# Depthwise convolution in 16x4 cells, a LayerNorm centred in PSUM, and the mixer weights loaded from GpSimd's queue

## The reference

```
x  [8, 96, 64, 64] float32
h  = batch_norm1(x)                                   # per channel scale and shift
h  = depthwise conv 17x17, padding 8, 96 groups
h  = 1x1 conv (96 x 96), batch_norm2, exact gelu
h  = h * squeeze_excite(mean of h over the image)
x1 = x + gamma * h
xn = layer_norm over the 96 channels of x1, with gain and offset
out = mamba(xn) + flip(mamba(flip(xn)))               # 192 inner channels, 16 states, 4096 steps
```

## Time and profile before

| | |
|---|---|
| median of 3 runs | 5830.08 us (5827.94 to 5831.29) |
| the profiled execution | 5833.66 us, span 5831.9 us |
| mean granted TensorE clock | 0.761 of full |
| convolution ends (last copy into hs) | 513.4 us |
| pointwise: SP's first DMA | 513.67 us |
| normalise: SP's first DMA | 639.20 us |
| scan: SP's first DMA | 825.68 us |

### The profile page before, as it was taken

One profiled execution on the slowest core, in us unless ns is written; L12 is line 12 of the kernel. 1 busy time (PEld: TensorE's weight loads), 2 busy tenths in 40 slices (PEclk: granted clock), 3 DMA queues, 4 the chain that ended last, 5 costly groups with the idle time before them and its releaser, 6 DMA issues. The chain is left out here.

```text
span 5831.9 us, 75897 instructions
## 1 busy us (share of the span) xinstructions
PE 4650.0 (80%) x18020; PEld 1375.0 (24%) x18020; DVE 5255.8 (90%) x3583; ACT 3228.0 (55%) x5273; POOL 4947.2 (85%) x2349
## 2 busy tenths in 40 slices
PE   7998766777877888788788778787887878888877
PEld 5775311111111111111111111111111111111111
DVE  3322658999999999999999999999999999999998
ACT  1123755555565656655555655656556555556564
POOL 0000248999999999999999999999999999999998
PEclk9998886666677777777777777777777777777777
DMA  1011655555656666666666566665566666566666
GB/s 36 25 29 48 194 157 188 188 184 192 200 193 202 204 191 200 197 199 194 203 201 207 191 199 206 192 199 195 196 201 197 200 207 197 196 202 202 192 198 203
DMA packets 363220, 1050.78 MB, mean 180 GB/s; under 512 B 70868, under 2 KB 120294, under 8 KB 312604
## 3 DMA queue, kind: packets, MB, share of 16 engines
q1 hardware_dynamic: 354972, 1034.97, 55.5%
q10 hardware_dynamic: 8064, 14.16, 0.7%
HBM read 837.23 MB, written 211.63 MB: 180 GB/s over the span
## 5 line engine op out<-in xcount | busy, mean ns | idle before, releaser
L1405 POOL TENSOR_TENSOR hc<-hring,c_rep 128x1024 f32<-128x1024 f32 x1541 | 3599.7, 2360 | 74.7 <-DVE hring L1360 71.0
L1360 DVE TENSOR_TENSOR_SCAN hring<-decay,carry,u_ps 128x1024 f32<-128x1024 f32 x1221 | 2823.6, 2335 | 0.0
L1111 PE MATMUL u_ps<-stack_b,w_spread 48*128 48x512 bf16 x2442 | 995.4, 496 | 1005.3 <-DVE hring L1360 1001.4
L1342 DVE TENSOR_TENSOR u_ps<-u_ps,u_rep 128x1024 f32<-128x1024 f32 x1221 | 1478.0, 1211 | 72.6 <-DMA u_rep<-u_scr 55.6
L1236 ACT ACTIVATE decay<-dt_rep,w_a 128x1024 f32<-128x1024 f32 x1222 | 1396.4, 1145 | 224.4 <-DVE hring L1360 211.8
L1129 PE MATMUL y_ps<-hc,w_gather 128*32 128x512 f32 x6144 | 1131.9, 819 | 0.0
L1236 ACT ACTIVATE u_ps<-dt_rep,w_a 128x1024 f32<-128x1024 f32 x322 | 359.3, 1116 | 1102.6 <-DVE hring L1360 1102.2
L1392 POOL TENSOR_TENSOR drive_p<-u_rep,b_rep 128x1024 f32<-128x1024 f32 x322 | 760.4, 2362 | 10.1 <-DMA u_rep<-u_scr 10.1
L1360 DVE TENSOR_TENSOR_SCAN hring<-u_ps,carry,drive_p 128x1024 f32<-128x1024 f32 x321 | 752.0, 2343 | 0.0
L1111 PEld LDWEIGHTS u_ps<-stack_b,w_spread 48*128 48x128 bf16 x2442 | 144.9, 100 | 2369.6 <-DVE hring L1360 2168.7
L684 POOL TENSOR_TENSOR xs<-xc_ln,rs 96x512 f32<-96x512 f32 x64 | 89.9, 1405 | 707.1 <-ACT rs L668 693.4
(11 more groups left out here) (128 smaller groups left out, 4326.0 us busy)
## 6 DMA issues: line engine op xcount, KB each, us to landing
dt_rep<-dt_scr SPq DMA_DIRECT2D x194, 1024.0 KB, 5.8
u_rep<-u_scr SPq DMA_DIRECT2D x194, 1024.0 KB, 7.9
c_rep<-bc_scr SPq DMA_DIRECT2D x260, 512.0 KB, 4.9
b_rep<-bc_scr SPq DMA_DIRECT2D x130, 512.0 KB, 4.3
xn<-xn_scr SPq DMA_DIRECT2D x132, 384.0 KB, 5.2
y_scr<-y_sb SPq DMA_DIRECT2D x768, 64.0 KB, 2.0
xn<-xn_scr SPq DMA_DIRECT2D x132, 256.0 KB, 4.7
dt_scr<-dt_sb SPq DMA_DIRECT2D x260, 128.0 KB, 2.2
```

The lines of the kernel that those rows point to most:

```text
L1111: mm = nc.tensor.matmul(u_ps[nv % NSLOT][:, sl], w["spread"][:, q, :], upper(stack_b[drv][:, sl]), start=True, stop=True)
L1342: nc.vector.tensor_tensor(slot[:, :], slot[:, :], u_rep[r][:, b, :], ALU.mult).then_inc(drive_ready, 1)
L1360: nc.vector.tensor_tensor_scan(hring[nv % NHR][:, ::step], factor[:, ::step], term[:, ::step], carry[:, drv, nv:nv + 1], ALU.mult, ALU.add ...
L1405: nc.gpsimd.tensor_tensor(hc[nv % NHC][:, :], hring[nv % NHR][:, :], c_rep[q][:, :], ALU.mult).then_inc(c_applied, 1)
```

## The change

Three parts.

**Convolution by cells.** The output is made in cells of 16 rows by 4 columns. A stationary matrix then has 64 columns (16 rows x 4 columns of output) instead of 128, and 5 of them (`CELLS`) serve a channel in place of 9. The partitions of the input now stand for (column mod 4, 32 rows: 16 and a halo of 8 on both sides), and the four row blocks (`NCY`) lie on the free axis. Each of the 5 steps does two matmuls, for even and odd row blocks, into partitions 0 to 63 and 64 to 127 of PSUM. The band matrices need only 16 rows x 2 halves = 32 small matmuls for a batch. For this layout `x_cols` is not changed. Instead SP issues 12 DMAs for a batch: for each of the two inner row blocks two DMAs of 64 partitions, whose source is `[2 parities, 32 rows, 1024]`, and for each of the two edge blocks four DMAs of 24 partitions. Every row is 4 KB as before. The batch norm becomes 24 instructions on 64 partitions for a batch (L316), since rows outside the image need scale and shift of zero. ScalarE alone copies out of PSUM. GpSimd copies the bf16 halves of the taps (`part`), and GpSimd zeroes parts of `xraw` before the first load.

**Mixer loads.** The 62 loads go from SP's queue to GpSimd's.

**Normalise.** TensorE multiplies by `centrer` = identity - averager, so that the centred value arises in PSUM (`px`). ScalarE squares from there, and VectorE does `px * gain * rs` in one instruction and adds the offset in another. GpSimd has no work left in this block. The leads are other ones.

```diff
+CY, CX = 16, 4
+ROWS = CY + 2 * PAD
+CELLS = 2 * PAD // CX + 1
+CELL = CELLS * CX
+NCY = H // CY
+NEAR = CELLS // 2
+XC = W // CX
+XP = XC + 2 * NEAR
 YG = 4
-NYG = H // YG
+NYG = CY // YG
...
+                rows = d["x_cols"].rearrange("(a y) c b x -> a y (c b x)", a=2)
+                def load(buf, at):
+                    for q in range(NCY):
+                        first = q * CY - PAD
+                        lo, hi = max(0, first), min(H, first + ROWS)
+                        if hi - lo == ROWS:
+                            for k in range(2):
+                                sp.dma_start(xraw[buf][2 * ROWS * k:2 * ROWS * (k + 1), q, :], rows[:, lo:hi, bass.ds(at, CB * B * XH)]).then_inc(x_in[buf], 16)
+                        else:
+                            for k in range(4):
+                                to = ROWS * k + lo - first
+                                sp.dma_start(xraw[buf][to:to + hi - lo, q, :], rows[k % 2, lo:hi, bass.ds(at, CB * B * XH)]).then_inc(x_in[buf], 16)
+                sp.wait_ge(raw_zero, 1)
                 for i in range(2):
-                    sp.dma_start(xraw[i][:, :, :, :], xk[:, i * CB:(i + 1) * CB, :, :]).then_inc(x_in[i], 16)
+                    load(i, i * CB * B * XH)
...
+                pool.wait_ge(wide_ready, 5)
+                def take(s, buf):
+                    nc.gpsimd.tensor_copy(part[buf][:, :, :], upper3(wide[:, :, bass.ds(s * (CB * CELL), CB * CELL)])).then_inc(part_ready, 1)
+                take(0, 0)
+                take(1, 1)
+                with pool.Fori(0, BATCHES // 2) as i:
                     for par in range(2):
+                        pool.wait_ge(w_ready, NYG * (2 * i + par + 1))
+                        take(2 * i + par + 2, par)
...
+                def evacuate_weights(s, buf, yg, batches_before):
+                    bank = yg % 2
+                    if batches_before is not None:
+                        act.wait_ge(conv_done[buf], CB * batches_before)
+                    act.wait_ge(w_ready, NYG * s + yg + 1)
+                    src = pw[bank][:, 0:YG * CB * CELL].rearrange("p (y n o) -> p y n o", y=YG, o=CX)
+                    to = toep[buf][:, :, yg * YG * CX:(yg + 1) * YG * CX].rearrange("p n (y o) -> p y n o", o=CX)
+                    nc.scalar.copy(to, src).then_inc(w_evac[bank], 1)
...
+                        for c in range(CB):
+                            evacuate_weights(s + 1, 1 - par, c, i + par)
+                            act.wait_ge(conv_done[par], CB * i + c + 1)
+                            nc.scalar.copy(hs[:, bass.ds((CB * s + c) * B * XH, B * XH)], pc[c][:, 0:B * XH]).then_inc(h_evac[c], 1)
...
                 def batch_norm(s, buf, loads):
-                    dve.wait_ge(x_in[buf], 16 * loads)
+                    dve.wait_ge(x_in[buf], 16 * X_DMAS * loads)
                     for c in range(CB):
                         at = s * CB + c
-                        last = nc.vector.tensor_scalar(xpad[buf][:, c, :, NEAR:NEAR + XH], xraw[buf][:, c, :, :],
-                                                       scale[:, bass.ds(at, 1)], shift[:, bass.ds(at, 1)], ALU.mult, ALU.add)
+                        for h in range(2):
+                            rows = slice(64 * h, 64 * h + 64)
+                            src = xraw[buf][rows, :, :].rearrange("p q (c b x) -> p q c b x", c=CB, b=B)
+                            for k, cells in enumerate((slice(0, 1), slice(1, NCY - 1), slice(NCY - 1, NCY))):
+                                last = nc.vector.tensor_scalar(xpad[buf][rows, c, cells, :, NEAR:NEAR + XC], src[:, cells, c, :, h::2],
+                                                               scale[rows, k, bass.ds(at, 1)], shift[rows, k, bass.ds(at, 1)], ALU.mult, ALU.add)
                     last.then_inc(x_ready, 1)
...
+                        for h in range(2):
+                            last = nc.tensor.matmul(pw[bank][64 * h:64 * h + 64, r * CB * CELL:(r + 1) * CB * CELL],
+                                                    bands[:, yg * YG + r, :, :].rearrange("p a y -> p (a y)"),
+                                                    part[buf][:, h, :],
+                                                    start=True, stop=True, skip_group_check=True)
                     last.then_inc(w_ready, 1)
...
-                            for k in range(SHIFTS):
-                                n0 = (c * SHIFTS + k) * 2
-                                last = nc.tensor.matmul(pc[c][:, 0:B * XH].rearrange("p (b x) -> p b x", b=B),
-                                                        toep[par][:, n0:n0 + 2, :].rearrange("p a y -> p (a y)"),
-                                                        xpad[par][:, c, :, k:k + XH],
-                                                        start=(k == 0), stop=(k == SHIFTS - 1))
-                                if k % 2 == 1:
-                                    weights(s + 1, after[c][k // 2])
+                            for k in range(CELLS):
+                                for q in range(2):
+                                    last = nc.tensor.matmul(pc[c][64 * q:64 * q + 64, 0:B * XH].rearrange("p (f b x) -> p f b x", f=2, b=B),
+                                                            toep[par][:, c * CELLS + k, :],
+                                                            xpad[par][:, c, q::2, :, k:k + XC],
+                                                            start=(k == 0), stop=(k == CELLS - 1))
+                                if k == 2:
+                                    weights(s + 1, 1 - par, c)
                             last.then_inc(conv_done[par], 1)
...
-                for dst, src in mixer.loads:
-                    sp.dma_start(dst, src).then_inc(w_loaded, 16)
...
+            @block.gpsimd
+            def _(pool):
+                for dst, src in mixer.loads:
+                    pool.dma_start(dst, src).then_inc(w_loaded, 16)
...
+                        b, f, x = g // GPB, g % GPB // 4, g % 4
                         last = nc.tensor.transpose(pt[g % 2][0:C, r * P:(r + 1) * P],
-                                                   hs[:, :].rearrange("p (c n) -> p c n", c=C)[:, :, 4 * g + r], ident[:, :])
+                                                   hs[:, :].rearrange("p (c n) -> p c n", c=C)[:, :, (f * B + b) * XC + 4 * x + r], ident[:, :])
...
-                    nc.scalar.activation(act_out[b % 2][:, :, 8 * col:8 * col + 8].rearrange("c y x -> c x y"),
-                                         pp[g % 2][0:C, :].rearrange("c (x y) -> c x y", y=H), ACT.Gelu,
+                    f, x = col // 4, col % 4
+                    nc.scalar.activation(act_out[b % 2][:, 32 * f:32 * f + 32, 16 * x:16 * x + 16].rearrange("c y (r o) -> c r y o", o=CX),
+                                         pp[g % 2][0:C, :].rearrange("c (r y o) -> c r y o", r=4, o=CX), ACT.Gelu,
                                          bias=bt[:, 3:4], scale=bt[:, 2:3], accum_out=sums[:, g:g + 1]).then_inc(gelu_done, 1)
...
+                dve.wait_ge(ln_const, 64)
+                nc.vector.tensor_tensor(centrer[:, :], one[:, :], averager[:, :], ALU.subtract).then_inc(centrer_made, 1)
...
-                def centre(b, s):
+                def scale(b, s):
                     r = s % RING
-                    dve.wait_ge(mean_ready, NS * b + s + 1)
-                    dve.wait_ge(added, NS * b + s + 1)
-                    after(dve, scaled, NS * b + s - RING + 1)
-                    nc.vector.tensor_tensor(xc[:, r, :], x1[:, r, :], pm[s % NM][0:C, :], ALU.subtract).then_inc(centred, 1)
-                def gain(b, s):
+                    dve.wait_ge(rs_ready, NS * b + s + 1)
+                    after(dve, affine, NS * b + s - RING + 1)
+                    nc.vector.scalar_tensor_tensor(xs[:, r, :], px[s % NX][0:C, :], lng[:, 0:1], rs[:, r, :],
+                                                   ALU.mult, ALU.mult).then_inc(scaled, 1)
+                def shift(b, s):
                     r = s % RING
                     dve.wait_ge(scaled, NS * b + s + 1)
                     after(dve, stored[r], 16 * (NS // RING * b + s // RING))
-                    nc.vector.tensor_scalar(xo[:, r, :], xs[:, r, :], lng[:, 0:1], lng[:, 1:2], ALU.mult, ALU.add).then_inc(affine, 1)
-                over_slices(dve, (4, add), (3, centre), (0, gain))
+                    nc.vector.tensor_scalar(xo[:, r, :], xs[:, r, :], lng[:, 1:2], None, ALU.add).then_inc(affine, 1)
+                over_slices(dve, (5, add), (1, scale), (0, shift))
...
+                def centre(b, s):
                     pe.wait_ge(added, NS * b + s + 1)
-                    after(pe, centred, NS * b + s - NM + 1)
-                    nc.tensor.matmul(pm[s % NM][0:C, :], averager[:, :], x1[:, s % RING, :], start=True, stop=True).then_inc(mean_ready, 1)
+                    after(pe, scaled, NS * b + s - NX + 1)
```

(19 more changed lines are left out.)

169 lines of the change are left out of this document (86 added, 83 removed).

## The result

The changed kernel takes 5912.7 us (median of 4 runs, 5912.16 to 5913.1), the kernel before 5830.68 us in the same session: a ratio of 1.014, 95% interval 1.0127 to 1.0153. It is slower by 82 us. The forecast was 5896 us.

What follows compares the result with a forecast made beforehand. Before, TensorE bounds the convolution; after, two DMA engines carrying the inner loads were to. 5833.7 + 104 (convolution) - 21 (pointwise) - 17 (normalise) = 5899.7, less 3.6 for the median: 5896 us; 5875 to 5955 holds eight in ten.

Steps and rivals of the forecast that it cites:

- Two DMA engines for the inner loads: Convolution loads: the source's outer dimension of 2 leaves each inner load two DMA engines, at 26 GB/s each.
- The convolution's term, +104: Convolution: 26 batches at 23.0 us, set by the loads, start the next stage at 617.8 instead of 513.67 us.
- For a batch each of them moves 4 x 32 + 8 x 2 = 144 packets: Convolution loads: each of the two DMA engines moves 0.59 MB, 22.7 us at 26 GB/s, taken as 23.0.
- rival (2): Convolution loads: slower packets, 19.3 GB/s as with all 16 engines, 205 us more, 6101 us; chance 5%.
- TensorE's batch, 10.5 us: Convolution: TensorE needs about 10.5 us for a batch, the matmuls for the two PSUM halves overlapping.
- rival (4): Convolution: TensorE at 1.2 GHz while waiting for loads; 21 us still hides behind 23, changing nothing; chance 2%.
- VectorE's batch, 6 us: Convolution: VectorE's 24 instructions for a batch take 6 us beside TensorE, 10 us at most.
- rival (1): Convolution: inner loads get many DMA engines, TensorE sets 10.5 us for a batch, 5576 us in all; chance 10%.
- every engine idle for two periods: Sign at the convolution's end: SP waits for x_in with every engine idle for two periods (23 us each).
- Pointwise, -21: Pointwise: ScalarE's stall of 18.42 us and slow groups behind it go, -21 us; GpSimd's queue costs 0 to +31.
- Normalise, -17: Normalise: 64 slices each 0.27 us shorter, -17 us, between -25 and +5.
- I take 2.27: Normalise: 2.27 us for a slice against 2.54 before, chosen since DMA then runs at 260 GB/s.

Runs made afterwards that it cites:

- experiment 1: Changed kernel with each inner load of 64 rows (source 2 x 32) issued as two loads of 32 rows, one parity each: 5536.96 us, ratio 0.949.
- experiment 3: Changed kernel with the first edge block's four loads of 24 rows each cut into 23 rows and 1: 6267.46 us (one run).
- experiment 8: Changed kernel without the edge blocks' loads in the loop, made for the first two batches only: 5822.49 us, ratio 0.9984 to the kernel before.
- experiment 5: Kernel before with only the 62 mixer loads moved from SP's queue to GpSimd's: 5805.09 us, ratio 0.996.
- experiment 7: Kernel before with normalise's multiply xc * rs moved from GpSimd to VectorE, centring still a subtraction on VectorE: 5835.89 us, ratio 1.0011.
- experiment 6: Kernel before with the new normalise alone, first slice loads ahead of two stores of zeros: 5800.57 us, ratio 0.9951.
- experiment 2: Changed kernel with only one of the two inner row blocks loaded by single parities, the other left at 2 x 32: 5740.70 us (one run).
- experiment 4: Changed kernel with the four inner loads of a batch issued from GpSimd's queue, edge loads left on SP: 5721.15 us (one run).

## Why the prediction was right, and where it was off

**Two DMA engines for the inner loads: right.** Experiments 1 and 3 move the divisor in both directions, from 2 to 16 (376 us gained) and from 12 to 1 for one block (355 us lost), with the bytes unchanged. The windows show 52 and 26 GB/s where the forecast had one figure of 26 for each.

**The convolution's term, +104, was +130.8: mis-sized.** The step that failed is "For a batch each of them moves 4 x 32 + 8 x 2 = 144 packets" at one price. The 128 inner packets cost what it says (experiment 8). The 16 edge packets were priced at 0.157 us and took 0.23. At 318 us the row has a share of 0.67, which is 10.7 DMA engines, and 209 GB/s: 19.5 for each, or 0.21 us for a packet. What fills the last 0.02 is not shown. 19.5 is the rate of the earlier trace rows with all engines at work, which the prediction had kept only as a bound for the whole batch, with the reason that "nothing else moves meanwhile"; for the edge loads' share of a batch this reason fails. At 24.0 us the sum closes: 18.5 + 26 x 24.0 + 1.3 = 643.8, against 644.48. Of the miss of 26.8 us, 26 come from a batch of 24.0 us in place of 23.0. For the whole batch at the slow rate, rival (2), there was nothing: with two engines alone it never occurs.

**TensorE's batch, 10.5 us: near.** Where it bounds, in experiment 1, it is 9.5 us. In the changed kernel it hides behind the loads. The two halves of PSUM overlap as forecast: the timeline of the kernel after has 20 records, a channel's, in 2.40 us.

```profile
297.93 2.40 PE L361 MATMUL pc<-xpad,toep 128*64 128x256 f32 x20
...
316.01 2.83 PE L361 MATMUL pc<-xpad,toep 128*64 128x256 f32 x12 [12.26 <-DVE xpad L316]
```

The second row is rival (4). After idling for 12.26 us TensorE runs at a granted clock of 0.50, its lower level of 1.2 GHz, and its first 12 records take 2.83 us; from 320 to 321 us it is granted 0.89 in the mean (windows above). It costs nothing behind a load of 24 us, as said.

**VectorE's batch, 6 us: mis-sized and without effect.** It is 7.58 us. The instructions with 128 elements per partition take 347 ns in the mean, against 411 with 256, so half the size saved only a sixth. In experiment 1 it is 80% of the period, no longer far from the bound.

**The loads spread, rival (1), 5576 us: did not happen,** but experiment 1 shows what it would have been worth, 5537.

**The signs.** The share of 0.22 and 77 GB/s, VectorE's waits for xraw and the falling clock came as named, and TensorE is busy for 51.62 of 100 us, a little more than the "less than half". One sign is wrong: "every engine idle for two periods" at the end. VectorE works on the 25th load too, until 628 us, so all engines stand idle for some 16 us and not 48 (windows of the kernel after):

```profile
630.00:640.00 10.00, 0.00 (x0) 0.00 (x0) 0.00 (x0) 0.00 (x0) 0.00 (x0) 0.50 0.19 68
```

**Pointwise, -21: right.** The stall's wait is gone and the stage is 22.5 us shorter, 21.2 in experiment 5. GpSimd's queue was the open cost, with bounds of 0 and 31 us. It starts at 645.03 us and issues the last four loads at 675.00 (timeline of GpSimd in the kernel after):

```profile
645.03 0.71 POOL L496 DMA_DIRECT2D w_in<-in_w_in  x1 [52.40 <-POOLq L177]
...
646.75 0.52 POOL L496 DMA_DIRECT2D taps<-in_conv_taps  x1
...
675.00 2.37 POOL L496 DMA_DIRECT2D a_log<-in_a_log  x4
```

That is 62 loads in 32.3 us, 0.52 for each where 1.53 would still have been hidden; the 1.31 us between groups of ScalarE didn't change. The Trainium skill, DMA: Bandwidth & Descriptors, section "Anatomy of one DMA — SWDGE (gpsimd) path", gives about 2 us fixed for a DMA there. The trace agrees with it as a landing time: the loads land 1.8 to 3.1 us after their issue in the median of each kind, only the 16 of a_log 4.3. These times don't add up, since the next issue doesn't wait for them, and the 29 us that the prediction named for that case did not come.

**Normalise, -17, was -30.4: mis-sized.** The step that failed is "I take 2.27" for a slice, chosen for the DMA. It ran at 2.1 us, as the timeline of VectorE in the kernel after shows.

```profile
807.71 0.75 DVE L685 SCALAR_TENSOR_TENSOR xs<-px,lng,rs 96x512 f32<-96x512 f32 x1 [0.27 <-ACT rs L733]
...
814.12 0.75 DVE L685 SCALAR_TENSOR_TENSOR xs<-px,lng,rs 96x512 f32<-96x512 f32 x1 [0.36 <-ACT rs L733]
```

Three slices take 6.41 us, 2.14 each. The DMA engines did not hold it: they moved 289 GB/s from 750 to 800 us, where the prediction had set the pace by 260, and VectorE's waits are for ScalarE (26.1 us in the stage) and hardly for a load (3.3). The prediction's other figures, VectorE's 2.0 us and the chain's 2.15, were the nearer ones. VectorE's three instructions are 0.742 + 0.747 + 0.474 = 1.96 us, and the slices shown have waits of 0.27 and 0.36 us for ScalarE's rs. The multiply from PSUM costs 747 ns, so the bound of +5 never came near; the result lies outside the term's other bound, -25. A second term was put at nothing, the start of the stage. The first adds, in the kernel before and in the one after:

```profile
648.40 0.75 DVE L611 SCALAR_TENSOR_TENSOR x<-h_in,gate,x_in_ln 96x512 f32<-96x512 f32 x1 [9.03 <-DMA x_in_ln<-in_x_tok]
...
753.67 0.75 DVE L678 SCALAR_TENSOR_TENSOR x<-h_in,gate,x_in_ln 96x512 f32<-96x512 f32 x1 [2.57 <-DMA x_in_ln<-in_x_tok]
```

They stand 9.2 and 6.1 us after the stage's first DMA. So 64 x 0.40 = 25.6 us come from the pace and 3.1 from the start; 1.7 stay open. SP now issues the first loads ahead of two stores of zeros, which is the likely reason for the 3.1 but was not tried alone. Experiment 7 shows one source of the gain: the end of the work on GpSimd, which had stretched VectorE's, pays for most of one more instruction of VectorE. What is gained beyond that (experiment 6 against 7, 35 us) is the instruction less on VectorE, by centring in PSUM, together with the other leads and the earlier first loads; these were not tried apart.

**The parts add up, and two misses cancel in part.** The convolution came out 26.8 us longer than forecast and normalise 13.4 shorter, so the total is nearer to the forecast (16.7 us) than its largest term; that is luck. Experiments 5 and 6 gave -25 and -30, the changed kernel's stages -22.5 and -30.4. In experiment 5 the untouched normalise stage came out 5 us shorter than before, in experiment 7 the untouched convolution and pointwise within 1 us: some 5 us of a stage with GpSimd and VectorE side by side is not to be read as an effect.

**Open.** The shared packets of experiment 2 cost 0.30 us, more than the edge packets of the changed kernel (0.23). The windows show a lower rate for each DMA engine there, 14.1 GB/s with all 16 at work against 19.5 with some 11. But with all 16 has 19.3, so the number at work is not the whole reason, and what else it is was not settled. Nor was it settled how much of experiment 4's time is GpSimd's order and how much its small packets.

## What to carry to other kernels

Before costing a load by its bytes, write down the outermost dimension of both its sides: from SP's queue the DMA engines that share it were, in every row here, the largest number up to 16 that divides them, always the same ones (several such loads queued together still ran at 52 GB/s). Here a `[2, 32, n]` source cost 376 us against two `[32, n]` loads. Price a packet by the company it has (0.16 us with two DMA engines at work, 0.21 to 0.30 with many), since the fullest engine sets the time. And count a part of GpSimd's work beside VectorE as VectorE's too: 90 us of multiplies there made VectorE's adds and gains 28 us longer, and moving them over cost 6 us in all.
